# A graph layer's second sums: 31 of 49 blocks of counts as float32r in two 12-bit pieces, the rest as bf16 in three

## The chip, the cores and the metric
The kernel runs on one core of one Trainium2 chip. Its time is the device time of an execution in microseconds (us); lower is better. The engines are called as in the profile: PE (TensorE matmul) and PEld (its weight loads), DVE (VectorE), ACT (ScalarE), POOL (GpSimd) and SP (SyncE, which here only issues DMAs).

## The reference
Two graph layers on 6250 nodes of 128 features and 200,000 edges sorted by destination:

```python
h = relu(layernorm(x))
x = x + L0(h)      # mean aggregation, twice, then a layernorm
h = relu(layernorm(x))
x = x + L1(h)      # attention over the edges, with edge attributes
# inside L0, with agg(h) = segment_sum(h[src], dst) / max(count, 1)
h1 = relu(agg(h) @ W1l.T + h @ W1r.T + b1)
h2 = agg(h1) @ W2l.T + h1 @ W2r.T + b2
return layernorm(h2 + x) * gamma + beta
```

What matters here is the second aggregation, agg(h1) @ W2l.T. It is computed as agg(h1 @ W2l.T): a sum of 128 numbers over the edges of each node.

## The kernel before, in words
Nodes lie in 49 blocks of 128. The kernel has six stages, one after the other: front, count_sums, hidden, product_and_norm, attention, finish.

**Counts.** count_sums turns the edges into 62 slabs (NSL = N_BLK + NOV = 49 + 13; the 13 cover the edges that a block has beyond its share). A slab is a matrix of 49 blocks of 128 x 128 small integers, how often a source node of a block occurs among the edges of a destination; as bf16 it is 1568 KB. It is used for the first sums and stored in a_tab, a table in device memory.

**Second sums.** product_and_norm reads the slabs again and multiplies each block with that block's node sums. To keep float32 accuracy with bf16 matmuls, hidden splits each node's 128 values (po, in PSUM) into three bf16 pieces, SPL[:, h, 0..2], five DVE instructions for two blocks (finish, L1248 on). A slab is then 49 matmuls (L1666) with a block of counts as weights and the 3 x 128 columns of pieces moving, all adding into one PSUM bank of psR; DVE adds the three pieces up (rows, L1689), one reduction of 128 x 384 per slab.

The slabs live in two buffers A[0] and A[1]. SP loads a slab two ahead, in halves: blocks 0 to 24 (L1413) when PE has used these of the slab before last (s_hf), the rest (L1415) when PE is through with it (s_pr). In slabs 4 to 16 SP also stores a row block of r_tab (L1424) and waits until it has landed, before it goes on to the next slab.

Beside the 49 matmuls PE has small work at fixed places of a slab: at block 8 the transposes of edge terms (turn_edges, L1613), at 24 combine (slabs 1 to 13), at 30 the blocks of chunks (blocks_of_chunks, L1618 and L1619, which wait for GE of DVE's chunk_blocks) or the transposes of chunks (L1624), at 40 turn (L1595, waits for V) and weigh (L1603, waits for HT).

Destinations are normalized four blocks at a time. For the slab after such a quad (i == ends[q] + 1) DVE runs normed(q): it adds the overflow rows, means, statistics, then waits for ACT's square root, for ACT's U (norm, L1501), and for a second square root, before it reduces the slab. ACT then makes V (L1508). In the first 27 slabs, except these, DVE also computes an edge tile (edges, L1813 and L1816, four times each). POOL gathers the overflow rows and the chunks' rows, ACT also issues loads and stores of x.

Each engine runs its list strictly in the order written; semaphores order them against each other. attention gathers a row of x_tab for each edge on POOL (L1987), 15 chunks of 128 edges at a time.

Of the kernel before, what the change touches and what calls it, by code (L numbers as in the profile page):

```python
# [23 lines left out]
I16 = mybir.dt.int16  # L24
ACT = mybir.ActivationFunctionType
# [3 lines left out]
P = 128  # L29
# [5 lines left out]
QUAD = 4  # L35
# [39 lines left out]
UN_S, UNITS = 16, P // 16  # L75
NV = N_BLK * P
# [53 lines left out]
def build(nc, x, src, dst, edge_attr, W1l, W1r, b1, W2l, W2r, b2, gamma, beta,  # L130
          W, W_edge, att_src, att_dst, att_edge, bias, out):
    with ExitStack() as top:
# [20 lines left out]
        kinds[s_pq.num] = True  # L153

# [5 lines left out]
        ae_t = nc.dram_tensor("ae_t", [P, HEADS, NK], F32).ap()  # L160
        a_tab = nc.dram_tensor("a_tab", [NSL, P, N_BLK * P], BF16).ap()
# [12 lines left out]
        BLK = sb("BLK", [1, N_GRP + 2, 16], I16)  # L174
# [9 lines left out]
        ACC = sb("ACC", [P, NB, MW])  # L184
# [3 lines left out]
        W1T = sb("W1T", [P, 2, D_HID], F32, XS)  # L188
        W2T = sb("W2T", [P, 2, 2, D], F32, XS)
# [6 lines left out]
        identb = sb("identb", [P, P], BF16, XS)  # L196
        EKI = sb("EKI", [P, NPR + NOV], I32, XS)
        LEN = sb("LEN", [P, NPR + NOV], F32, XS)
        SECOND = sb("SECOND", [P, NPR], F32, XS)
        H = sb("H", [P, NB, XW], F32, XS)  # L200
        SPL = sb("SPL", [P, NB, 3, D], BF16, XS)
        lastp = sb("lastp", [P, 1], F32, XS)
        MB = sb("MB", [P, HEADS, D_EDGE], F32, XS)
        VAL = sb("VAL", [P, N_BLK, 4], F32, XS)
        OVI = sb("OVI", [P, N_BLK], I32, XS)
# [5 lines left out]
        flat_c = ACC[:].rearrange("p b f -> p (b f)")  # L211
# [21 lines left out]
        def front(at, block):  # L233
# [45 lines left out]
            zr = flat_c[:, NB * D:NB * D + 4 * P]  # L279
# [126 lines left out]
            def _(pool):  # L406
# [5 lines left out]
                pool.memset(zr, 0.0).then_inc(s_io, 1)  # L412
# [143 lines left out]
            def _(dve):  # L556
# [4 lines left out]
                dve.memset(BLK[:], 0)  # L561
# [171 lines left out]
        def count_sums(at, block):  # L733
# [246 lines left out]
            def _(dve):  # L980
# [39 lines left out]
                def rows(i):  # L1020
                    t = order[i]
                    if t < N_BLK:
                        to = ACC[:, t, 0:D]
# [17 lines left out]
                def behind(k):  # L1041
# [4 lines left out]
                    a = ACC[:, QUAD * k:high, 0:D]  # L1046
# [39 lines left out]
                dve.memset(ACC[:, N_BLK:, 0:D], 0.0)  # L1086
# [24 lines left out]
        stage(count_sums)  # L1111


        def hidden(at, block):
# [127 lines left out]
            def _(dve):  # L1242
                def mean(t, u):
                    dve.tensor_tensor(A2[:, u], ACC[:, bass.ds(t * PAIR, PAIR), 0:D],
                                      RCNT[:, bass.ds(t * PAIR, PAIR)][:, :, None].to_broadcast([P, PAIR, D]),
                                      ALU.mult).then_inc(s_a, 1)

                def finish(t, u):  # L1248
# [4 lines left out]
                    c.mark(dve.tensor_copy(SPL[:, pair, 0], o[:, :, 0]))  # L1253
# [4 lines left out]
                    dve.tensor_tensor(Y2[:, u], o[:, :, 0], SPL[:, pair, 0], ALU.subtract).then_inc(s_y, 1)  # L1258
                    dve.wait_ge(s_y, t + 3)
                    c.link(dve.tensor_copy(SPL[:, pair, 1], Y2[:, u]))  # L1260
                    c.mark(dve.tensor_tensor(SPL[:, pair, 2], Y2[:, u], SPL[:, pair, 1], ALU.subtract))
# [7 lines left out]
                def step(t, u):  # L1269
                    dve.wait_ge(s_t, t + 2)  # L1270
                    mean(t + 3, 1 - u)
                    finish(t, u)
                looped = (NP2 - 3) // HU * HU
                with dve.Fori(0, looped // HU) as i:
                    for u in range(HU):
                        step(HU * i + u, u % 2)
                for t in range(looped, NP2 - 3):
                    step(t, t % 2)
                for t in range(NP2 - 3, NP2):
                    finish(t, t % 2)  # L1280
# [5 lines left out]
        def product_and_norm(at, block):  # L1286
# [5 lines left out]
            s_hf = sem("q_hf", at)  # L1292
            s_gc = sem("g_c", at)
# [9 lines left out]
            s_pr = sem("q_pr", at)  # L1303
# [45 lines left out]
            rows3 = sb("rows3", [P, 2, 3, P], I32, at)  # L1349
            rowsf = sb("rowsf", [P, 3, P], F32, at)  # L1350
            dstf = sb("dstf", [P, P], F32, at)
            blk_row = sb("blk_row", [1, NK], I16, at)
# [6 lines left out]
            X = sb("X", [P, 3, QUAD, D], F32, at)  # L1359
# [39 lines left out]

            def width(q):  # L1400
# [6 lines left out]
            def _(sp):  # L1407
                for i, t in enumerate(order):
                    tile = a_tab[t].rearrange("p (h s) -> p h s", h=N_BLK)

                    if i >= 2:
                        sp.wait_ge(s_hf, i - 1)
                        sp.dma_start(A[i % 2][:, 0:HALF], tile[:, 0:HALF]).then_inc(s_ld[2 * (i % 2)], 16)  # L1413
                        sp.wait_ge(s_pr, i - 1)
                        sp.dma_start(A[i % 2][:, HALF:], tile[:, HALF:]).then_inc(s_ld[2 * (i % 2) + 1], 16)  # L1415
                    for n in range(KC):
                        if i == columns[n] + 6:
# [4 lines left out]
                    if 0 <= o < NOV:  # L1422
                        sp.wait_ge(s_rp, o + 1)
                        sp.dma_start(r_tab[o * P:(o + 1) * P], RP[:, o % 2]).then_inc(s_rt, 16)  # L1424
                        sp.wait_ge(s_rt, 16 * (o + 1))

# [1022 lines left out]
```

## Time and profile before

| | us |
|---|---|
| median of 3 runs | 4843.48 |
| lowest and highest | 4829.29, 4848.03 |
| span of the profiled execution, first to last instruction | 3640.9 |
| the second sums in it, first to last matmul (L1666) | 982.6 to 1539.8 |
| attention's gathers (L1987), from | 1557.05 |
| PE busy in the span | 3010.1 (83%) |
| DVE, POOL, ACT busy | 2616.2 (72%), 1928.6 (53%), 1004.4 (28%) |

The profiler gives the span from the first to the last instruction; it has no row for the rest of an execution's time. Matmuls are pipelined: the duration of one includes its way through the array, so their pace is read from the distance of their starts, or from a merged row as (duration - that of one) / (count - 1). Idle time ahead of an instruction stands in brackets with what ended it. The granted clock (PEclk) is 1.00 at 2.4 GHz and 0.50 at 1.2 GHz.

### The profile page before, as it was taken

To read this page: it belongs to the slowest core of one execution; us is meant where nothing else is said; L and a number is where in the kernel's file an instruction comes from. 1 tells how busy PE (TensorE), PEld (TensorE's weight loads), DVE (VectorE), ACT (ScalarE), POOL (GpSimd) and SP (SyncE) were. 2 spreads that over 40 slices of the span, in tenths; PEclk is the share of its full clock that TensorE was granted. 3 is DMA by queue.
4 is the path that set the end of the run, shared out by engine and by line. 5 is a ranking of instruction groups with operands and counts; after the bars stand their busy time and mean duration, and the time that the engine had idled before them with its cause. 6 is when DMAs were issued, how large, how long until landed. Compare 5 with 4: busy or idle time off the path is not lost. (4 is left out here: it accounts for less than half of the span.)

```text
span 3640.9 us, 66661 instructions
## 1 busy us (share of the span) xinstructions
PE 3010.1 (83%) x21816; PEld 2408.1 (66%) x21816; DVE 2616.2 (72%) x7465; ACT 1004.4 (28%) x2323; POOL 1928.6 (53%) x1970
## 2 busy tenths in 40 slices
PE   5799999999999999988777777777777777777774
PEld 5566666777765566567676666766666676666673
DVE  4789999996587644477676666676666676666677
ACT  4455555565300111122222212222222222211220
POOL 5430110162102233167777777777777777777773
PEclk9999999999999999967666666666666666666666
DMA  5233333474178788632222222222222222222225
GB/s 167 84 133 143 133 149 132 151 169 149 44 225 234 213 245 250 185 96 55 56 55 55 56 55 56 55 55 56 55 56 55 55 56 55 56 55 55 55 55 96
DMA packets 150358, 378.62 MB, mean 104 GB/s; under 512 B 38934, under 2 KB 87630, under 8 KB 141634
## 3 DMA queue, kind: packets, MB, share of 16 engines
q0 software_dynamic: 66640, 129.84, 17.8%
q1 hardware_dynamic: 41974, 217.22, 16.4%
q10 hardware_dynamic: 41372, 26.95, 2.5%
q8 instruction: 191, 3.13, 0.4%
q14 instruction: 181, 1.48, 0.1%
HBM read 255.77 MB, written 119.69 MB: 103 GB/s over the span
## 5 line engine op out<-in xcount | busy, mean ns | idle before, releaser
L1987 POOL DMA_INDIRECT G<-x_tab,idx x1611 | 1529.5, 949 | 501.4 <-issue 489.4
L2076 PE MATMUL pu<-MSG,OH 128*128 128x140 f32 x3282 | 626.6, 353 | 2.0 <-DVE ACC L2173 2.0
L2173 DVE TENSOR_TENSOR ACC<-pu,ACC 128x140 f32 x1641 | 485.2, 296 | 131.7 <-PE pu L2076 85.4
L931 PE MATMUL psR<-SPL,AE 128*128 128x384 bf16 x3038 | 569.5, 328 | 0.0
L2076 PEld LDWEIGHTS pu<-MSG,OH 128*128 128x128 f32 x3282 | 559.4, 246 | 5.5 <-DVE ACC L2173 2.0
L1666 PE MATMUL psR<-SPL,AE 128*128 128x384 bf16 x3038 | 511.9, 328 | 3.1 <-PEq L216 2.3
L2007 ACT COPY OHT<-pt 128x512 f32<-128x512 f32 (+1 forms) x432 | 236.9, 558 | 955.9 <-PE pt L2052 954.8
L898 ACT CAST AE<-psA 128x784 bf16<-128x784 f32 x496 | 397.6, 813 | 319.6 <-PE psA L921 318.2
L2065 PE MATMUL px<-ADG,OHT 128*128 128x4 f32 x3240 | 463.6, 270 | 0.0
L2065 PEld LDWEIGHTS px<-ADG,OHT 128*128 128x128 f32 x3240 | 435.6, 211 | 10.4
L1666 PEld LDWEIGHTS psR<-SPL,AE 128*128 128x128 bf16 x3038 | 297.7, 98 | 195.9 <-issue 7.4
L2098 PE MATMUL pc<-ident,L 128*60 128x128 f32 x108 | 42.2, 390 | 450.1 <-DVE L L2240 450.1
L1013 DVE TENSOR_TENSOR OHL<-iol,LH 128x1024 bf16<-128x1024 bf16 (+1 forms) x496 | 397.1, 801 | 22.6 <-PE psA L921 19.3
L931 PEld LDWEIGHTS psR<-SPL,AE 128*128 128x128 bf16 x3038 | 275.0, 98 | 146.2 <-issue 5.2
L2052 PE MATMUL pt<-ident,OH 128*128 128x128 f32 x1620 | 356.6, 381 | 11.0 <-ACT OHT L2007 9.2
L2098 PEld LDWEIGHTS pc<-ident,L 128*60 128x60 f32 x108 | 13.6, 126 | 482.9 <-issue 482.9
L2052 PEld LDWEIGHTS pt<-ident,OH 128*128 128x128 f32 x1620 | 284.1, 202 | 59.2 <-ACT OHT L2007 33.9
L921 PEld LDWEIGHTS psA<-OHH,OHL 128*128 128x128 bf16 x4800 | 234.5, 98 | 97.9 <-DVE OHH L1013 47.1
L921 PE MATMUL psA<-OHH,OHL 128*128 128x98 bf16 (+1 forms) x4800 | 262.4, 201 | 31.7 <-DVE OHH L1013 31.2
L1013 DVE TENSOR_TENSOR OHH<-iol,LH 128x784 bf16<-128x784 bf16 (+1 forms) x496 | 280.1, 565 | 0.0
L2233 DVE TENSOR_TENSOR L<-G,AE 128x60 f32<-128x60 f32 x108 | 27.8, 258 | 328.2 <-DMA G<-x_tab,idx 327.7
L853 POOL DMA_INDIRECT srows<-src_pad,EKI x38 | 51.1, 1344 | 397.9 <-DVE KB L996 343.7
(415 smaller groups left out, 3544.3 us busy)
## 6 DMA issues: line engine op xcount, KB each, us to landing
a_tab<-AE SPq DMA_DIRECT2D x62, 1568.0 KB
AE<-a_tab SPq DMA_DIRECT2D x60, 800.0 KB, 6.0
AE<-a_tab SPq DMA_DIRECT2D x60, 768.0 KB, 6.2
G<-x_tab,idx POOLq DMA_INDIRECT x1611
at_in<-in_edge_attr SPq DMA_DIRECT2D x26, 250.0 KB
room<-in_edge_attr ACTq DMA_DIRECT2D x24, 250.0 KB
ae_t<-room ACTq DMA_DIRECT2D x13, 256.0 KB, 5.4
AE<-ae_t SPq DMA_DIRECT2D x1, 3328.0 KB, 11.5
```

Source lines behind the costliest of these rows:

```text
L898: act.copy(A[i % 2][:, :, UN_S * u:UN_S * (u + 1)].rearrange("p h (k s) -> p k h s", k=2), psA[:, n % 2, :, 0:W8].rearrange("p k (s h) -> ...
L921: mm = pe.matmul(psA[:, n % 2, c * w // W8, to:to + w], OHL[:, n % 4, c], OHH[:, n % 4, c * step:c * step + w], start=True, stop=True)
L931: mm = pe.matmul(psR[:, i % 2, 0:3 * D], A[i % 2][:, h, :], SPL[:, h].rearrange("p s f -> p (s f)"), start=(h == 0), stop=(h == N_BLK - 1))
L1013: return dve.tensor_tensor(out.rearrange("p (s h t) -> p s h t", s=k, t=2), iol[:, 0:w].rearrange("p (h t) -> p h t", t=2)[:, None].to_bro ...
L1666: mm = pe.matmul(psR[:, i % 2, 0:3 * D], A[i % 2][:, h, :], SPL[:, h].rearrange("p s f -> p (s f)"), start=(h == 0), stop=(h == N_BLK - 1))
L1987: pool.indirect_dma_start(G[:, u % 4, j, :], None, x_tab, bass.IndirectOffsetOnAxis(ap=idx[:, u % 4, j:j + 1], axis=0)).then_inc(s_g[u % 4 ...
L2007: act.copy(OHT[:, 4 * n:4 * n + w, :].rearrange("p a b -> p (a b)"), pt[:, n % 2, 0:w * P]).then_inc(s_te, 1)
L2052: mm = pe.transpose(pt[:, n % 2, (j % 4) * P:(j % 4 + 1) * P], OH[:, u % 4, j, :], ident[:])
L2065: mm = pe.matmul(px_l[:, :, j], OHT[:, j, :], ADG[:, j, :], start=True, stop=True)
L2076: mm = pe.matmul(pu[:, k[0], k[1]:k[1] + MW], OH[:, u % 4, j, :], MSG[:, u % 2, j, :], start=True, stop=True)
L2098: pe.transpose(pl, L[:].rearrange("p h j -> p (h j)"), ident[:]).then_inc(s_lt, 1)
L2173: dve.tensor_tensor(a, pu[:, k[0], k[1]:k[1] + MW][:, None, :], a, ALU.add).then_inc(s_c, 1)
```

## The change
- hidden writes the pieces of the first 18 blocks as before (`three`, into SPB). For the other 31 it writes two pieces as float32r (`two`, into SPR): the value with its low 12 bits cleared, by shifts on the integer view, and the rest. Both have 12 bits of significand, so a product with a small integer is exact in either.
- product_and_norm: ACT casts the counts of blocks 18 to 48 from bf16 to float32r, in four groups a slab (7, 8, 8, 8 blocks), into one of three buffers AR. PE multiplies the blocks 0 to 17 as before (384 columns), the others from AR with 256 moving float32r columns; both add into psR. The order in a slab is six bf16 blocks, group 0, six, group 1, six, group 2, group 3, with the small work between them.
- The second half of a slab is now loaded when ACT has cast it; the first still waits for PE's s_hf, now behind block 17 and group 1.
- In the slab after a quad ACT puts the next slab's casts 0 and 1 between U and the second square root, and cast 2 between that and V.
- To make room, rows3 has one buffer, rowsf, X and zr lie elsewhere, ACC is split (SUMS before attention), and blk_row goes through a table blk_tab: 13 small stores on SP, one strided load and a memset on POOL at the start of attention. The four semaphores of attention's gathers are kept from the start of the kernel.

```diff
+N_BF = 18
+N_FR = N_BLK + N_BLK % 2 - N_BF
...
+                def two(t, u, r):
...
+                    o = po[:, u].rearrange("p (n l o) -> p n l o", n=PAIR, l=2)
+                    c = Chain(dve, own, t, 3)
+                    dve.wait_ge(s_o, t + 3)
+                    c.mark(dve.tensor_scalar(Y2[:, u].bitcast(I32), o[:, :, 0].bitcast(I32), 12, 12,
+                                             ALU.arith_shift_right, ALU.logical_shift_left))
+                    dve.wait_ge(s_b, t + 1)
+                    h = H[:, bass.ds(t * PAIR, PAIR), 0:D]
+                    c.link(dve.tensor_tensor(h, o[:, :, 1], h, ALU.add))
+                    pair = bass.ds(r * PAIR, PAIR)
+                    dve.tensor_tensor(SPR[:, pair, 1], o[:, :, 0], Y2[:, u], ALU.subtract).then_inc(s_y, 1)
+                    c.mark(dve.tensor_copy(SPR[:, pair, 0], Y2[:, u]))
...
+            groups = [range(N_BF, HALF)] + [range(h, h + 8) for h in range(HALF, N_BLK, 8)]
...
                         sp.wait_ge(s_hf, i - 1)
                         sp.dma_start(A[i % 2][:, 0:HALF], tile[:, 0:HALF]).then_inc(s_ld[2 * (i % 2)], 16)
-                        sp.wait_ge(s_pr, i - 1)
+                        sp.wait_ge(s_cs, 4 * (i - 1))
                         sp.dma_start(A[i % 2][:, HALF:], tile[:, HALF:]).then_inc(s_ld[2 * (i % 2) + 1], 16)
                     for n in range(KC):
+                        if i == columns[n] + 4:
+                            sp.wait_ge(s_bk, n + 1)
+                            sp.dma_start(blk_tab[:, n * P:(n + 1) * P], blk_row[:, n % 2]).then_inc(s_bs[n % 2], 16)
...
+                def cast(i, g):
+                    n = 4 * i + g
+                    if i >= 2 and g <= 1:
+                        act.wait_ge(s_ld[2 * (i % 2) + g], 16 * (i // 2))
+                    if n >= 3:
+                        act.wait_ge(s_cu, n - 2)
+                    rows_ = groups[g]
+                    act.copy(AR[:, n % 3, 0:len(rows_)], A[i % 2][:, rows_[0]:rows_[-1] + 1]).then_inc(s_cs, 1)
...
+                    normed = [q for q in range(NQ - 1) if i == ends[q] + 1]
+                    for q in normed:
+                        first_norm(q)
+                    if i + 1 < NSL:
+                        cast(i + 1, 0)
+                        cast(i + 1, 1)
+                    for q in normed:
+                        sqrt(2 * q + 1)
+                    if i + 1 < NSL:
+                        cast(i + 1, 2)
+                    for q in normed:
+                        second_norm(q)
...
+                def cast(i, g):
+                    n = 4 * i + g
+                    pe.wait_ge(s_cs, n + 1)
+                    for k, h in enumerate(groups[g]):
+                        mm = pe.matmul(psR[:, i % 2, 0:2 * D], AR[:, n % 3, k],
+                                       SPR[:, h - N_BF].rearrange("p s f -> p (s f)"), start=False,
+                                       stop=(h == N_BLK - 1))
+                    mm.then_inc(s_cu, 1)
...
+                    counted(i, range(0, 6))
+                    beside(i, 8)
+                    cast(i, 0)
+                    counted(i, range(6, 12))
+                    beside(i, 24)
+                    cast(i, 1)
+                    counted(i, range(12, N_BF)).then_inc(s_hf, 1)
+                    beside(i, 30)
+                    cast(i, 2)
+                    beside(i, 40)
+                    cast(i, 3)
...
-                    dve.wait_ge(s_pr, i + 1)
+                    dve.wait_ge(s_cu, 4 * (i + 1))
```

## Rows read from the trace of the kernel before

**Rows 1.** Stretches: busy us (instructions) per engine, PEclk, DMA share, GB/s
```profile
982.00:1121.00 139.00, 138.44 (x860) 85.87 (x861) 116.10 (x246) 0.00 (x0) 9.78 (x10) 0.99 0.70 228
1121.00:1234.00 113.00, 101.97 (x602) 62.12 (x600) 86.16 (x226) 11.66 (x30) 35.73 (x33) 0.95 0.79 216
1234.00:1541.00 307.00, 303.25 (x1913) 191.79 (x1911) 130.28 (x503) 39.84 (x98) 82.77 (x83) 1.00 0.80 231
1641.00:3550.00 1909.00, 1460.89 (x8993) 1317.26 (x8992) 1327.61 (x4391) 400.64 (x1334) 1445.11 (x1523) 0.68 0.25 55
```

**Rows 2.** Instructions of L1666: ns min/median/max, first and last start in us
```profile
L1666 PEld LDWEIGHTS psR<-SPL,AE x3038: 95/98/152, 982.5 to 1539.7; 128*128 128x128 bf16 x190
L1666 PE MATMUL psR<-SPL,AE x3038: 322/326/528, 982.6 to 1539.8; 128*128 128x384 bf16 x190
```

**Rows 3.** Waits, 982 to 1545: us in total, times, longest
```profile
DVE ACC L1689 <- PE psR L1666: 159.6, 32, 7.7
PE psg L1618 <- DVE GE L1774: 7.5, 10, 2.9
```

**Rows 4.** Timeline of PE, merged: start, us, operation, count, idle before
```profile
895.35 1.89 PE L1217 MATMUL po<-W2T,HID 128*128 128x256 f32 x8
897.07 0.27 PE L1199 MATMUL pt<-ident,A 128*128 128x128 f32 x1
897.18 0.27 PE L1200 MATMUL pt<-ident,H 128*128 128x128 f32 x1
...
1405.23 0.38 PE L1618 MATMUL psg<-dq,GE 49*128 49x2 f32 x2 [0.34 <-DVE GE L1774]
...
1417.31 10.89 PE L1666 MATMUL psR<-SPL,AE 128*128 128x384 bf16 x66
...
1584.57 3.41 PE L2065 MATMUL px<-ADG,OHT 128*128 128x4 f32 x30
```

**Rows 5.** Timeline of DVE, 1391 to 1427: reductions of four slabs
```profile
1391.29 0.56 DVE L1689 TENSOR_REDUCE ACC<-psR 128x128 f32<-128x384 f32 x1 [5.98 <-PE psR L1666]
...
1402.40 0.56 DVE L1689 TENSOR_REDUCE ACC<-psR 128x128 f32<-128x384 f32 x1
...
1418.97 0.56 DVE L1689 TENSOR_REDUCE ACC<-psR 128x128 f32<-128x384 f32 x1 [6.92 <-PE psR L1666]
...
1426.93 0.56 DVE L1689 TENSOR_REDUCE ACC<-psR 128x128 f32<-128x384 f32 x1 [5.97 <-PE psR L1666]
```

**Rows 6.** Instructions of L482 and of L1161, on ACT
```profile
L482 ACT CAST SPL<-H x7: 937/938/940, 59.4 to 102.4; 128x896 bf16<-128x896 f32 x7
L1161 ACT COPY H<-H x25: 400/402/405, 881.6 to 966.3; 128x256 f32 x20, 128x256 f32<-128x256 f32 x5
```

**Rows 7.** Timeline of ACT in the same period: the second square root
```profile
1401.47 0.30 ACT L1495 ACTIVATE sd<-nv,eps 128x4 f32<-128x4 f32 x1 [3.25 <-DVE nv L122]
```

**Rows 8.** DMA issues: count, KB each, median us from issue to landing
```profile
AE<-a_tab SPq DMA_DIRECT2D x60, 800.0 KB, 6.0
...
AE<-a_tab SPq DMA_DIRECT2D x2, 1568.0 KB, 8.1
```

**Rows 9.** Groups of DVE by line, 982 to 1121: busy us, mean ns
```profile
L1813 DVE TENSOR_TENSOR prod<-room,MB 125x512 f32<-125x512 f32 x64 | 44.1, 689 | 6.0 <-DMA room<-in_edge_attr 4.1 <-issue 0.3
```

**Rows 10.** Timeline of SP: issues of the r_tab store and of first halves
```profile
1053.07 0.78 SPq L1424 DMA_DIRECT2D r_tab<-RP  x1
1061.60 0.32 SPq L1413 DMA_DIRECT2D AE<-a_tab  x1
...
1069.61 0.32 SPq L1413 DMA_DIRECT2D AE<-a_tab  x1
```

**Rows 11.** Timeline of PE: weights that waited, and the matmuls behind them
```profile
1201.69 1.78 PE L1603 MATMUL pw<-WX,HT 128*128 128x136 f32 x8 [3.55 <-DVE HT L1729]
1203.27 15.60 PE L1666 MATMUL psR<-SPL,AE 128*128 128x384 bf16 x88
```

**Rows 12.** Costliest groups of the page: attention's gathers on POOL
```profile
L1987 POOL DMA_INDIRECT G<-x_tab,idx x1611 | 1529.5, 949 | 501.4 <-issue 489.4
```

More of the change, by code:

```diff
@@ L24 @@
 I16 = mybir.dt.int16
+F32R = mybir.dt.float32r
 ACT = mybir.ActivationFunctionType
@@ L153, in build @@
         kinds[s_pq.num] = True
+        s_src = [top.enter_context(nc.semaphore(f"row_g{u}")) for u in range(4)]
+        for h in s_src:
+            kinds[h.num] = True
         src_pad = nc.dram_tensor("src_pad", [E_PAD], I32).ap()
@@ L1111, in build @@
         stage(count_sums)
+        CS.close()
+        FS_ = ExitStack()
+        SPB = sb("SPB", [P, N_BF, 3, D], BF16, FS_)
+        SPR = sb("SPR", [P, N_FR, 2, D], F32R, FS_)
         def hidden(at, block):
@@ L1292, in product_and_norm @@
             s_hf = sem("q_hf", at)
+            s_cs = sem("q_cs", at)
+            s_cu = sem("q_cu", at)
+            s_bk = sem("q_bk", at)
+            s_bs = [sem(f"q_bs{k}", at) for k in range(2)]
             s_gc = sem("g_c", at)
@@ L1398, in product_and_norm @@
             LAST_I = NSL - 1
+            groups = [range(N_BF, HALF)] + [range(h, h + 8) for h in range(HALF, N_BLK, 8)]
+            assert len(groups) == 4 and groups[-1][-1] == N_BLK - 1
             def width(q):
@@ L1425, in _ @@
                         sp.wait_ge(s_rt, 16 * (o + 1))
+                for k in range(2):
+                    sp.wait_ge(s_bs[k], 16 * ((KC - k + 1) // 2))
             @block.gpsimd
@@ L1549, in _ @@
                 load(1)
+                for g in range(3):
+                    cast(0, g)
                 for i in range(NSL):
+                    cast(i, 3)
                     if i - 1 in at_tile:
@@ L1880, in attention @@
             assert N_GRP % UN == 0
-            s_g = [sem(f"a_g{u}", at, gathers=True) for u in range(4)]
+            s_g = s_src
             s_i = sem("a_i", at)
@@ L1978, in _ @@
                 sp.dma_start(AE[:], ae_t).then_inc(s_ael, 16)
+                sp.wait_ge(s_bz, 1)
+                with nc.allow_non_contiguous_dma(reason="groups of 15 numbers"):
+                    sp.dma_start(BLK[:, 2:N_GRP + 2, 0:J], blk_tab[:, 0:N_GRP * J].rearrange("o (g j) -> o g j", j=J)
+                                 ).then_inc(s_bl, 16)
             @block.gpsimd
@@ L1989, in step @@
                                 ap=idx[:, u % 4, j:j + 1], axis=0)).then_inc(s_g[u % 4], 16)
+                pool.memset(BLK[:], 0).then_inc(s_bz, 1)
                 steps(pool, step)
```

175 lines of the change are left out of this document (96 added, 79 removed).

## The prediction
> **What bounds the kernel now.** The change touches one stage in earnest, the second sums, so the profile is read there. First the stretches [rows 1]: the stage is cut where its load changes, and the reader should compare the engines within a row. From 982 to 1121 us (slabs 0 to 15) PE is busy throughout and DVE for 116 of 139. From 1121 to 1234 (slabs 16 to 26) PE has holes, DVE is at 76%. From 1234 to 1541 (slabs 27 to 61) PE is busy for 303 of 307, DVE for 42%. The DMA engines are busy 0.70 to 0.80 of it. Then the line view of the stage's matmuls [rows 2]: 3038, that is 49 for each of 62 slabs, starting at 982.6 and ending at 1539.8, 557 us. Last the waits [rows 3]: the reduction that closes a slab waits for PE 32 times, 160 us, while PE's longest item is 7.5 us. So PE bounds the stage, with DVE close behind while edge tiles last.
>
> **The price of a matmul.** The old form: 66 in 10.89 us, the last taking 0.33 to end, so (10.89-0.33)/65 = 0.1625 apart [rows 4]. A slab is 49 x 0.1625 = 7.96, also the step between two undisturbed reductions, 1418.97 to 1426.93 [rows 5]. The new form, float32r with 256 columns, is not in the trace. Nearest rows [rows 4]: float32 with 256 columns, issued as two matmuls each, (1.89-0.38)/7 = 0.216 apart, twice what 256 columns take at the pace of the 384; float32 transposes, 128 columns in one go, 0.11; float32 matmuls of only 4 columns, (3.41-0.27)/29 = 0.108. The last two, with 128 and 4 columns at the same step, show what a float32 weight load costs when nothing longer covers it. So one pass at a column a cycle gives 0.11 (columns 0.108, load 0.11, side by side); two cycles a column, as in each float32 pass, give 0.216; two such passes 0.432. I take 0.11, since cutting values to 12 bits only has a use if the form skips passes, and keep 0.216 as a rival; the gain cannot exceed that of 0.11.
> The Trainium skill (FP8 and Floating Point Precision, TensorE Precision Notes) has four passes for true float32 and a reduced-precision reading of it, cut to 22 bits; it does not name float32r nor its pace, and no row here shows it. If that reading is this form, a quarter of 2 x 0.216 is 0.108, the same sum.
> A new slab: 18 x 0.1625 + 31 x 0.11 = 2.93 + 3.41 = 6.34 us, 1.62 less. Times 62 that is 100 us, a ceiling. It is not reached, for a different reason in each stretch.
>
> **The casts.** ScalarE gets four per slab, of 896 and three times 1024 elements. Its nearest rows are a cast of 896, 0.938, and a copy of 256, 0.402 [rows 6]: 0.84 ns an element, 1.05 us for 1024, so 4.1 a slab, beside some 40 us of its own in the last 307 [rows 1]. Capacity is there. It runs in order, though, and has three buffers, so it is three groups ahead of PE at most, and around the normalization it is busy answering DVE. Bounds: nothing, or a cast behind V in each period, some 3 us.
>
> **Third stretch, a period of four slabs.** Now 1391.29 to 1426.93 = 35.65 us [rows 5]: 31.84 of counts, 3.8 of transposes, weights and small matmuls. Call the first reduction 0; PE then starts the slab of the normalization. New: that slab ends at 6.4. DVE's chain keeps its length: the second square root at 10.2 [rows 7], the next reduction at 11.1 [rows 5]. In the second slab PE comes to the blocks of chunks (L1618) at about 11.6, but GE is written after that reduction; today PE starts L1618 2.8 us after it and has waited 0.34 [rows 4, 5]. So it starts at 13.9, a stall of 2.3. The cast of group 2 (12.2), V (13.8) and the cast of group 3 (14.9) come under that cover. The slab ends at 16.9; the third, with weights and edge transposes, at 24.7; the fourth at 31.1. Period 31.4, gain 4.2.
> The same bytes move in less time: 0.80 of the stretch is busy DMA, so 0.85 or so of a full period, 30 us of 35.65; of 31.4 it would be 0.96. Half a tile lands 6.0 us after its issue, a whole one 8.1 [rows 8]; both halves are now asked for together at 72% of a slab, some 9 us ahead of need, enough while the queues are not full. Full gain is 4.2; queues held to 0.90 give a period of 33.8 and 1.9. I take 3.2, nearer the first because PE hardly waits for a tile now. Times 8.5 periods: 27 us.
>
> **First stretch.** Slabs take 8.5. DVE's 116.1/16 = 7.3 each is one floor, 5.5 of it the eight instructions of an edge tile [rows 1, 9]. SP's queue is the other. In slabs 4 to 16 SP asks for two halves, stores r_tab, and waits until that has landed behind their 1.6 MB: from the store at 1053.07 the next load is issued at 1061.60, and the next after that at 1069.61 [rows 10]. A turn of 8.0 to 8.9, whatever PE does. Those 13 slabs stay at 8.2, gain 0.3 each, 4; three before them gain 0.9; the first waits for its first cast. The blk_tab store adds an issue of 0.4 us on SP in some. In all 6 us.
> The Trainium skill (DMA: Bandwidth & Descriptors, Queues, rings and completion order) says that a semaphore increment lands only after every earlier write of that DMA engine. For this kernel r_tab would then wait for both halves in full; the 8.5 from 1053.07 to 1061.60 agrees, and a turn of 8.9 throughout would leave 2 of the 6.
>
> **Second stretch.** DVE sets its pace: three iterations in four hold an edge tile, the fourth the normalization (11.1 [rows 5]). Its slack is behind the weights, where PE stalls 3.55 for HT and then lost clock, 88 matmuls in 15.60 us instead of 14.6 [rows 11]. The group behind the weights becomes 0.88 from 1.47; PE's stall grows to 7 us and the clock is lost again. Gain 0.6 x 3, called 2.
>
> **Edits at little cost.** The hidden layer's DVE work shrinks (four instructions for five, 16 pairs), behind PE's matmuls of 0.216: nothing. BLK is loaded at the start of attention on SP, behind AE, while DVE clears its tiles; if that cover is gone DVE loses the lateness once. Its memset stands on POOL ahead of 1611 gathers, which at 949 ns and 0.30 of issue each make attention's length [rows 12]: +1 us (0 to 2). chunk_rows on POOL waits for rowsf of the chunk before, done two slabs before the wait in front of it: nothing. The load of X and the stores behind it on ScalarE's queue are issued up to two casts later, 2 us, with a period to spare.
>
> **The sum.** -27 -6 -2 +1 = -34 us, made on the profiled span, 3640.9 us. The median of the runs is 4843.5; the 1202.6 us between them lie around the span, no row shows them, and I hold them constant. 4843.5 - 34 = **4809.5**, 0.7% faster. A measurement of this kernel can tell about 0.5% (24 us) from no change.
>
> **Rivals.**
> 1. *The queues bind* (0.23). For it: 0.96 of the time in the sum above. Against it: PE hardly waits for tiles today. Third stretch 1.0 x 8.5, first 3, attention +1: 4833.
> 2. *Everything hides* (0.14). Queues give way, no stall but DVE's: third stretch 5.2 x 8.5 = 44, first 14, second 4, less 1: 4782.
> 3. *Two cycles a column* (0.10), on the slower side. A slab is 2.93 + 31 x 0.216 = 9.63, +1.67. Third stretch 34 x 1.67 = 57 and 5 of stalls; first, 16 x 1.7 = 27; second 10: +99, 4942. It decides from 0.163 per float32r matmul on. For it: each float32 pass of the trace. Against it: the use of the 12-bit cut.
> 4. *The clock* (0.06), also slower. In attention PE is busy for 1461 of 1909 us and has clock 0.68, in the third stretch 1.00 [rows 1]. Stalls in each period, and PE near 75% in the second stretch, could bring the lower level. A slab there costs up to twice 6.34, 4.7 more than now; the others gain 0.55, so it decides from 7 slabs of 62 on. With 20: 96 - 23 = +73, 4916.
> 5. *ScalarE is late* (0.05): 3 us more in each period: 4835.
>
> The forecast itself has 0.42, with 4795 to 4822 as its own range. The range for 8 in 10 reaches over rivals 2, 1 and 5: **4772 to 4856**. Faster by over 0.5%: 0.42 + 0.14 + the faster edge of rival 1 = 0.58; within 0.5%: 0.26; slower: rivals 3 and 4, 0.16.
>
> **What would show it.** Float32r matmuls 0.11 apart in PE's timeline (0.216: rival 3) and casts of 0.94 and 1.05 us. Reductions of the third stretch with a period near 32.4 and a stall at L1618's successor near 2.3; a period near 30 is rival 2, one of 34 with PE or ScalarE waiting for a_tab is rival 1. SP's turn in slabs 4 to 16 still 8 us or more. The second stretch as long as before. Attention the same within 2 us. It would be wrong most of all if the time around the span moved, or if the second sums lost their clock.

## The result and the profile after

| | us |
|---|---|
| before, median of 4 runs | 4836.39 (4829.00 to 4848.03) |
| after, median of 4 runs | 4800.85 (4794.29 to 4807.22) |
| ratio, with its 95% interval | 0.992 (0.990 to 0.994) |
| second sums after, first to last matmul | 1075.3 to 1603.3, 528.0 |
| second sums before [rows 2] | 557.3 |

The change is 0.8% faster, 35.5 us; 34 were forecast. The line view of the stage's matmuls, after (columns as in [rows 2]; L1742 are the bf16 blocks, L1750 the float32r ones), and below it ACT's casts:

```profile
L1750 PEld LDWEIGHTS psR<-SPR,AR x1922: 186/188/338, 1078.9 to 1603.2; 128*128 128x128 f32 x193
L1750 PE MATMUL psR<-SPR,AR x1922: 276/279/668, 1078.9 to 1603.3; 128*128 128x256 f32 x193
L1742 PE MATMUL psR<-SPB,AE x1116: 323/326/543, 1075.3 to 1601.4; 128*128 128x384 bf16 x186
...
L1561 ACT CAST AR<-AE x248: 920/1044/1054, 1078.0 to 1598.9; 128x896 fp32r<-128x896 bf16 x62, 128x1024 fp32r<-128x1024 bf16 x62
```

3038 matmuls as before, 31 of 49 in the new form. The three stretches of the stage after, in the form of [rows 1]:

```profile
1075.00:1221.00 146.00, 127.82 (x909) 102.33 (x909) 121.69 (x256) 66.46 (x68) 13.65 (x14) 0.98 0.67 226
1221.00:1326.00 105.00, 83.45 (x556) 66.99 (x557) 79.33 (x216) 53.81 (x74) 29.89 (x29) 0.93 0.83 224
1326.00:1603.00 277.00, 261.19 (x1905) 218.14 (x1904) 129.49 (x499) 172.05 (x233) 84.62 (x84) 0.98 0.84 255
```

PE, busy throughout the first stretch before, now has holes of 18 us in 146 there, though it has less to do: something else sets the pace. In the third it is still busy for 261 of 277. One period of the third stretch, the reductions in DVE's timeline (start, us; [rows 5] are their counterpart):

```profile
1402.92 0.56 DVE L1790 TENSOR_REDUCE SUMS<-psR 128x128 f32<-128x384 f32 x1 [4.73 <-PE psR L1750]
...
1414.04 0.56 DVE L1790 TENSOR_REDUCE SUMS<-psR 128x128 f32<-128x384 f32 x1
...
1421.38 0.56 DVE L1790 TENSOR_REDUCE SUMS<-psR 128x128 f32<-128x384 f32 x1 [4.55 <-PE psR L1750]
...
1429.77 0.56 DVE L1790 TENSOR_REDUCE SUMS<-psR 128x128 f32<-128x384 f32 x1 [5.97 <-PE psR L1750]
...
1436.32 0.56 DVE L1790 TENSOR_REDUCE SUMS<-psR 128x128 f32<-128x384 f32 x1 [4.49 <-PE psR L1750]
```

This period takes 33.4 us in place of 35.65; over seven periods the mean is 32.7. The 11.12 behind the first reduction is DVE's own chain, unchanged. PE's timeline in the slab behind it, merged as in [rows 4]:

```profile
1416.88 0.38 PE L1699 MATMUL psg<-dq,GE 49*128 49x2 f32 x2 [2.07 <-DVE GE L1875]
1417.12 0.47 PE L1700 MATMUL psg<-GE,ones 49*128 49x128 f32 x2
1417.52 1.26 PE L1750 MATMUL psR<-SPR,AR 128*128 128x256 f32 x8
1418.58 1.05 PE L1676 MATMUL pt<-ident,V 128*128 128x128 f32 x4
1419.28 2.06 PE L1750 MATMUL psR<-SPR,AR 128*128 128x256 f32 x8
```

Eight float32r matmuls take 1.26 us at the full clock; two microseconds behind the stall on GE they take 2.06, at the lower clock of 1.2 GHz. Last comes SP in the first stretch (issues of the two halves, L1462 and L1464, of blk_tab and of r_tab, L1476):

```profile
1142.19 0.32 SPq L1462 DMA_DIRECT2D AE<-a_tab  x1
1142.56 0.44 SPq L1464 DMA_DIRECT2D AE<-a_tab  x1
1143.04 0.43 SPq L1476 DMA_DIRECT2D r_tab<-RP  x1
1151.52 0.32 SPq L1462 DMA_DIRECT2D AE<-a_tab  x1
1151.88 0.43 SPq L1464 DMA_DIRECT2D AE<-a_tab  x1
1152.37 0.34 SPq L1468 DMA_DIRECT2D blk_tab<-blk_row  x1
1152.77 0.33 SPq L1476 DMA_DIRECT2D r_tab<-RP  x1
1160.83 0.32 SPq L1462 DMA_DIRECT2D AE<-a_tab  x1
```

A turn of SP, from one load of a first half to the next, is 9.3 us here; 8.5 of them lie between the r_tab store at 1143.04 and the next load at 1151.52. Over the 13 turns the mean is 8.9 us, in the change's second trace 8.6, and single turns take 6.6 to 10.3. The waits from 1105 to 1325 us name the victims (us in total, times, longest):

```profile
ACT AR L1561 <- DMA AE<-a_tab: 70.7, 29, 5.2
...
PE psR L1742 <- DMA AE<-a_tab: 10.0, 7, 3.0
```

**One table for all that follows**, in us, from each trace: the stage from first to last matmul, and the distance from the 4th reduction to the 17th, from the 17th to the 27th and from the 27th to the 61st. Slabs count from 0, so the first of these distances is the length of slabs 4 to 16, the ones with an r_tab store; in what follows the three columns are called the first, second and third stretch (they are nearly those of [rows 1], whose first also holds slabs 0 to 3). Where a kernel has more than one trace, all stand. The stage is the better measure of these edits: it is free of the other 4200 us.

| kernel | stage | 4 to 17 | 17 to 27 | 27 to 61 |
|---|---|---|---|---|
| before (three traces) | 557.3, 557.3, 563.1 | 110.8, 110.8, 110.8 | 105.0, 105.4, 110.6 | 298.1, 297.7, 298.2 |
| the change (two) | 528.0, 524.8 | 111.4, 107.9 | 105.0, 105.4 | 270.7, 270.8 |
| GE early | 512.5 | 105.7 | 106.9 | 259.1 |
| no landing wait | 516.4 | 99.7 | 101.8 | 274.1 |
| both (two) | 501.5, 504.5 | 102.2, 102.2 | 101.4, 104.6 | 257.3, 257.0 |
| no casts | 529.1 | 112.5 | 103.8 | 271.7 |
| three quarters of the bytes | 514.0 | 101.9 | 100.1 | 271.3 |
| one piece | 538.4 | 105.7 | 106.2 | 286.0 |
| both, 24 and 25 blocks | 506.2 | 101.2 | 103.6 | 260.0 |
| both edits on the kernel before | 555.8 | 110.8 | 108.2 | 293.4 |

In one and the same kernel the third stretch repeats within 0.5 us and the first within 3.5; the second moves by up to 5.6, so nothing is built on it. The kernels without casts, with three quarters of the bytes and with one piece leave out part of the sums; they are there for their traces, of which each has one.

### The profile page after: what moved, and what is told of

It reads as the page before. It is cut to its first block and busy times, and to the rows that moved or that the text cites. A ratio compares the mean times of both kernels' runs of the same rounds, so it can differ in the third digit from the quotient of the medians.

```text
span 4803.3 us, 67019 instructions
## 1 busy us (share of the span) xinstructions
PE 3358.5 (70%) x21816; PEld 2859.1 (60%) x21816; DVE 2595.9 (54%) x7447; ACT 1247.5 (26%) x2571; POOL 1920.3 (40%) x1971
## 5 line engine op out<-in xcount | busy, mean ns | idle before, releaser
L2175 PE MATMUL px<-ADG,OHT 128*128 128x4 f32 x3240 | 684.3, 324 | 422.3 <-issue 413.9
L2175 PEld LDWEIGHTS px<-ADG,OHT 128*128 128x128 f32 x3240 | 665.8, 296 | 410.0 <-issue 386.1
L2186 PEld LDWEIGHTS pu<-MSG,OH 128*128 128x128 f32 x3282 | 705.4, 303 | 7.4 <-DVE ACC L2283 2.3
L942 PE MATMUL psR<-SPL,AE 128*128 128x384 bf16 x3038 | 573.7, 330 | 0.0
L942 PEld LDWEIGHTS psR<-SPL,AE 128*128 128x128 bf16 x3038 | 276.1, 98 | 148.5 <-issue 8.8
L1750 PE MATMUL psR<-SPR,AR 128*128 128x256 f32 x1922 | 289.8, 296 | 11.6 <-ACT AR L1561 11.5
L1561 ACT CAST AR<-AE 128x896 fp32r<-128x896 bf16 x248 | 245.3, 1017 | 196.0 <-PE psR L1750 86.4
L1750 PEld LDWEIGHTS psR<-SPR,AR 128*128 128x128 f32 x1922 | 251.5, 193 | 27.5 <-ACT AR L1561 18.0
L2254 DVE TENSOR_TENSOR MSG<-G,pq 128x1920 f32<-128x1920 f32 (+1 forms) x109 | 231.7, 2126 | 16.8 <-issue 16.8
L2248 DVE TENSOR_TENSOR OH<-pq,REL 128x1920 f32<-128x1920 f32 x108 | 231.9, 2148 | 0.0
```

Of the source, the lines that this page charges most:

```text
L942: mm = pe.matmul(psR[:, i % 2, 0:3 * D], A[i % 2][:, h, :], SPL[:, h].rearrange("p s f -> p (s f)"), start=(h == 0), stop=(h == N_BLK - 1))
L1561: act.copy(AR[:, n % 3, 0:len(rows_)], A[i % 2][:, rows_[0]:rows_[-1] + 1]).then_inc(s_cs, 1)
L1750: mm = pe.matmul(psR[:, i % 2, 0:2 * D], AR[:, n % 3, k], SPR[:, h - N_BF].rearrange("p s f -> p (s f)"), start=False, stop=(h == N_BLK - 1))
L2175: mm = pe.matmul(px_l[:, :, j], OHT[:, j, :], ADG[:, j, :], start=True, stop=True)
L2186: mm = pe.matmul(pu[:, k[0], k[1]:k[1] + MW], OH[:, u % 4, j, :], MSG[:, u % 2, j, :], start=True, stop=True)
```

## The experiments

The theory: PE's shorter slabs brought out two waits that had cost the old kernel nothing, the one for GE behind DVE's chain in the third stretch, and SP's for the landing of r_tab in the first. The rivals are the DMA queues (bytes), ScalarE's casts, and the pace of the new form.

**The change again.**

> The changed kernel again, as it stands, to be compared with the three others of this call on the same chip. Expected 0.992 of the kernel before (35 us less), as in its first timing, with the second sums' third stretch at a period of 32.7 us and slabs 4 to 16 at 9.3 to 9.4 us for each turn of SP.

4803.68 us against 4837.71, ratio 0.993 (0.991 to 0.995). The third stretch repeats within 0.1 us, so differences of some us in it can be read. The first is 3.5 us shorter than in the first trace: SP's turn has a mean of 8.6 us, not the 9.3 to 9.4 expected.

**GE early.** DVE writes GE of the next chunk right after it has read this chunk's rows out of psg, ahead of the five instructions that make the keys and of that slab's other work.

```diff
-                    dve.tensor_tensor(LAST[:, k], dstf[:], psg[:, 3 * P:], ALU.not_equal)
+                    c.link(dve.tensor_tensor(LAST[:, k], dstf[:], psg[:, 3 * P:], ALU.not_equal))
+                    if n + 1 < KC:
+                        chunk_blocks(n + 1)
...
-                    for n in range(KC):
-                        if i == columns[n]:
-                            chunk_blocks(n)
+                    if i == columns[0]:
+                        chunk_blocks(0)
```

> GE is written as soon as DVE has read the transposed chunks out of PSUM, three instructions after the reduction instead of nine. Theory (DVE's late GE stalls PE in the second slab of a period): the stall of 2.1 us goes down to some 0.5, the lower clock behind it goes too, period 32.7 to about 30.7, so some 15 us less than the changed kernel. Rival (the DMA queues bind): period stays at 32.7. Rival (ScalarE is late): PE's stall moves to the cast of group 2 and at most 5 us are gained.

4784.07 us (4779.28 to 4788.42), 19.6 under the change; the stage is 12.3 to 15.5 us shorter (15 expected), the third stretch 11.7. PE's waits for GE in it, of the change and then of this kernel:

```profile
PE psg L1699 <- DVE GE L1875: 14.1, 7, 2.2
```

```profile
PE psg L1699 <- DVE GE L1875: 5.4, 7, 1.0
```

That is 8.7 us less. The change has three dips of the clock in that stretch, 3.4 us each at 1.2 GHz, which by an estimate at half the pace lose 1.7 us each; this kernel has none. 8.7 + 5.1 = 13.8, against 11.7 measured: a stall of 2 us costs itself and a dip now and then. The wait isn't gone, because GE still stands behind the reduction and three reads of psg; only the keys no longer come between.

**No landing wait.** Two semaphores for r_tab in place of one, so that SP need not wait for each store.

```diff
-            s_rt = sem("q_rt", at)
+            s_rt = [sem(f"q_rt{k}", at) for k in range(2)]
...
-                        sp.dma_start(r_tab[o * P:(o + 1) * P], RP[:, o % 2]).then_inc(s_rt, 16)
-                        sp.wait_ge(s_rt, 16 * (o + 1))
+                        sp.dma_start(r_tab[o * P:(o + 1) * P], RP[:, o % 2]).then_inc(s_rt[o % 2], 16)
...
```

> SP no longer waits for the landing of the r_tab store; two semaphores carry it to those who need it. Theory (SP's turn of 9.3 us bounds slabs 4 to 16): these slabs fall to DVE's floor of 7.1 to 7.6 us, about 22 us less than the changed kernel; the third stretch is unchanged. Rival (the queues' bytes bind there: 2.0 MB a slab): they stay above 8.8, at most 5 us less.

4785.62 us (4770.07 to 4796.37), 18 under the change. The first stretch takes 99.7, 8 to 12 less, or 7.7 a slab, where 7.1 to 7.6 and 22 us in all were expected. In these 99.7 us PE is busy for 96.6 and DVE for 93.4: both are near their limit, and PE's own work binds at least as much as DVE's. The third stretch, expected unchanged, is 3.4 us longer and has one dip of the clock more. ACT's and PE's waits for the table from 1105 to 1325 us:

```profile
ACT AR L1561 <- DMA AE<-a_tab: 35.8, 22, 2.6
...
PE psR L1742 <- DMA AE<-a_tab: 1.6, 1, 1.6
```

Half of ACT's wait for the table and nearly all of PE's is gone.

**Both.** The two edits together, and the same once more.

> Both edits of the two runs before together. If the two causes are separate the gains add: about 37 us less than the changed kernel, 0.984 to 0.985 of the kernel before. If the queues bind, less than the sum: 10 us or under.

> The version with both edits (GE early, no landing wait, 18 and 31 blocks) once more, in five rounds, since its timed gain over the change (26 us) was less than the 38 us that the two edits gave one by one, while its second sums had lost the whole 13 and 10 us. Theory: the stage holds 501 to 504 us and ends the last 34 slabs in 257, so the time is 56 us or more below the kernel before, a ratio of 0.988 where that takes 4806 to 4840 us and of 0.984 to 0.985 where it takes 3641. Rival: the two edits get in each other's way, then the gap to the kernel before stays under 50 us.

4777.47 us (4770.44 to 4783.65) against 4837.71, ratio 0.988 (0.986 to 0.990); the second time 4771.9 (4768.62 to 4780.85) against 4841.14, ratio 0.986 (0.983 to 0.989). The stage is at 501.5 and 504.5, 53 to 56 us under the kernel before, and in it the gains of the two edits simply add (12.3 to 15.5, and 8.4 to 11.6). Timed it is 60 and 69 us. This version beats both kernels. The expected 37 us under the change were too much: the stage gives 20 to 26, and 26 was measured. The 37 were the sum of the two timed gains, 19.6 and 18, and each of these is some us more than its stage shows; where the excess comes from is open.

**The kernel before, traced again.**

> The kernel before, profiled once more, since the first trace of it has a span of 3640.9 us and its timed runs are at 4836. If the profiled run was unlike the timed ones, the new span will be near 4830, with the difference in attention, whose groups took 18.7 us in the first trace and 28.9 in the changed kernel's. If the time lies around the span, the span stays at 3640. The second sums should take 557 us in either case.

The stage has 557.3 us a second time, to the tenth. Its span is 4764.2, so in length this execution is like the change's and not like the one that the prediction was made on. That is taken up below.

**No casts.** All casts but the first six are copies of one column; the counts of the float32r blocks are left out.

```diff
-                    act.copy(AR[:, n % 3, 0:len(rows_)], A[i % 2][:, rows_[0]:rows_[-1] + 1]).then_inc(s_cs, 1)
+                    if n < 6:
+                        act.copy(AR[:, n % 3, 0:len(rows_)], A[i % 2][:, rows_[0]:rows_[-1] + 1]).then_inc(s_cs, 1)
+                    else:
+                        act.copy(AR[:, n % 3, 0, 0:1], A[i % 2][:, rows_[0], 0:1]).then_inc(s_cs, 1)
```

> The casts are left out but for the first six; one column is copied in place of each, so the counts used for 31 blocks are wrong. Theory (casts are hidden under DVE's chain and GE's stall): third stretch 32.7 to 32 at most, first and second stretch unchanged. Rival (ScalarE late): period falls to 30 or less.

ACT's groups from 1070 to 1600 us: one cast now costs 0.19 us in place of 1.04, and the 242 short ones 42.9 us in all; the change's 248 casts take 247.0:

```profile
L1564 ACT CAST AR<-AE 128x1 fp32r<-128x1 bf16 x242 | 42.9, 189 | 356.7 <-PE psR L1753 180.4 <-DMA AE<-a_tab 153.2 <-issue 15.2
```

The stage stays: 529.1, the third stretch 271.7, and PE's waits for GE in it 13.6 us. 200 us of ScalarE's work are worth nothing in time. Rival 5 falls.

**Three quarters of the bytes.** The second half of a slab brings 12 of its 24 blocks; the others keep old counts.

```diff
-                        sp.dma_start(A[i % 2][:, HALF:], tile[:, HALF:]).then_inc(s_ld[2 * (i % 2) + 1], 16)
+                        sp.dma_start(A[i % 2][:, HALF:HALF + 12], tile[:, HALF:HALF + 12]).then_inc(s_ld[2 * (i % 2) + 1], 16)
```

> Each slab loads 37 of its 49 blocks; the other 12 keep what an earlier slab left, so sums are wrong. It takes a quarter of the bytes away. Theory: the third stretch keeps its period of 32.7 us within 0.7; SP's turn in slabs 4 to 16 falls from 9.3 to about 7.5, since the store lands behind fewer bytes. Rival (queues bind): the third stretch falls to 30 to 31.

The third stretch has 271.3, as with all bytes (270.7): rival 1 falls, the queues bind nothing there. The first stretch falls to 101.9, nearly as far as without the landing wait, which has all the bytes and takes 99.7. So the bytes cost time there only by way of SP's wait: what it waits for is the bytes ahead of r_tab's.

**One piece.** The float32r matmuls take 128 columns, the high piece alone; the low piece is left out of the sum.

```diff
-                        mm = pe.matmul(psR[:, i % 2, 0:2 * D], AR[:, n % 3, k],
-                                       SPR[:, h - N_BF].rearrange("p s f -> p (s f)"), start=False,
+                        mm = pe.matmul(psR[:, i % 2, 0:D], AR[:, n % 3, k],
+                                       SPR[:, h - N_BF, 0], start=False,
```

> The float32r matmuls take only the high piece, 128 columns instead of 256; the low piece is left out. It asks what sets their pace of 0.118 us. Weight load: still 0.11 to 0.118. Columns: 0.06. A form that is slow when short: 0.2 or more, and a slower stage.

PE's timeline of it: eight of the new form in 1.14 us, with their weights as in the change:

```profile
1396.47 1.14 PE L1750 MATMUL psR<-SPR,AR 128*128 128x128 f32 x8
...
1400.93 0.38 PE L1699 MATMUL psg<-dq,GE 49*128 49x2 f32 x2 [2.33 <-DVE GE L1875]
1401.17 0.47 PE L1700 MATMUL psg<-GE,ones 49*128 49x128 f32 x2
1401.57 1.39 PE L1750 MATMUL psR<-SPR,AR 128*128 128x128 f32 x8
1402.75 1.07 PE L1676 MATMUL pt<-ident,V 128*128 128x128 f32 x4
1403.48 1.95 PE L1750 MATMUL psR<-SPR,AR 128*128 128x128 f32 x8
```

The change takes 1.24 to 1.26 for eight. The median distance of starts is 0.113 us, for 0.118 with 256 columns: half the columns save 4%, so the second piece is all but free, and columns don't set the pace. Nor does each matmul have such a cost of its own: in the stage of the counts, with bf16 weights of the same 128 x 128, matmuls of 98 columns start 0.043 us apart in the median:

```profile
306.51 0.89 PE L921 MATMUL psA<-OHH,OHL 128*128 128x98 bf16 x16
```

Float32 with 4 and with 128 columns and float32r with 128 and with 256 all start 0.11 to 0.12 us apart ([rows 4] and here). That leaves the load of a float32 block of weights as what sets the pace.
And the kernel ends slower: the third stretch takes 286.0, 15 more than the change with twice the columns. The clock now falls behind each of the stretch's seven stalls on GE (the row at 1403.48), for 6.8 us each time, where the change has three falls of 3.4 us; in the whole stage it falls 17 times for 8 and 9 in the change. The stretch's granted clock is 0.90, the change's 0.98. The stalls on GE are nearly the same, 16.2 us in all for 14.1. Why the clock falls more often was not tried further.

**One size changed.** Both edits, with 24 and 25 blocks in place of 18 and 31 (`N_BF = 24`).

> The version with GE early and without the landing wait, but with 24 blocks in three bf16 pieces and 25 in two float32r pieces instead of 18 and 31. By the measured distances (0.1625 and 0.118 us) a slab costs 6 x 0.0445 = 0.27 us more. Theory: with both waits gone the stage follows PE's own work, so the last 34 slabs take 34 x 0.27 = 9 us more (257 to 266), the whole stage some 13 to 16 us more than 501.5 (about 516), the first stretch less than its full share, as DVE's edge tiles are near it. Rival: something else than PE's work sets the pace (queues, ScalarE's order): the stage stays within 3 us of 501.5. Another rival: a longer run of bf16 matmuls keeps the clock up better, then less than 9.

The stage takes 506.2, 2 to 5 more than the version with both edits, where 13 to 16 were expected; the third stretch 260.0, only 2.9 more, not 9. The reductions tell why. One period at 18 and 31 blocks, then at 24 and 25:

```profile
1384.39 0.56 DVE L1790 TENSOR_REDUCE SUMS<-psR 128x128 f32<-128x384 f32 x1 [4.63 <-PE psR L1750]
...
1395.52 0.56 DVE L1790 TENSOR_REDUCE SUMS<-psR 128x128 f32<-128x384 f32 x1
...
1400.50 0.56 DVE L1790 TENSOR_REDUCE SUMS<-psR 128x128 f32<-128x384 f32 x1 [2.21 <-PE psR L1750]
...
1408.45 0.56 DVE L1790 TENSOR_REDUCE SUMS<-psR 128x128 f32<-128x384 f32 x1 [5.53 <-PE psR L1750]
...
1415.00 0.56 DVE L1790 TENSOR_REDUCE SUMS<-psR 128x128 f32<-128x384 f32 x1 [4.56 <-PE psR L1750]
```

```profile
1296.76 0.56 DVE L1790 TENSOR_REDUCE SUMS<-psR 128x128 f32<-128x384 f32 x1 [4.90 <-PE psR L1750]
...
1307.88 0.56 DVE L1790 TENSOR_REDUCE SUMS<-psR 128x128 f32<-128x384 f32 x1
...
1312.87 0.56 DVE L1790 TENSOR_REDUCE SUMS<-psR 128x128 f32<-128x384 f32 x1 [2.21 <-PE psR L1750]
...
1321.09 0.56 DVE L1790 TENSOR_REDUCE SUMS<-psR 128x128 f32<-128x384 f32 x1 [4.14 <-PE psR L1750]
...
1327.97 0.56 DVE L1790 TENSOR_REDUCE SUMS<-psR 128x128 f32<-128x384 f32 x1 [4.90 <-PE psR L1750]
```

The third and fourth slab cost 0.27 and 0.33 more, the share that the pace gives. The first two take 11.1 + 5.0 in both: there DVE's chain and GE behind it hold PE, and the longer blocks fill what was a wait. In the third stretch PE's waits for GE fall from 5.3 to 0.6 us and those for casts from 1.7 to 0.3; of 34 x 0.27 = 9.2 us that leaves 3.1, beside 2.9 measured. With both edits in, half of the periods' slabs are DVE's, and a still cheaper matmul would win only in the other half.

**Both edits on the kernel before.** GE early as above; SP waits for the store of the slab before, not for its own, so that a store has a slab's time to land.

```diff
+                        if o:
+                            sp.wait_ge(s_rt, 16 * o)
                         sp.dma_start(r_tab[o * P:(o + 1) * P], RP[:, o % 2]).then_inc(s_rt, 16)
-                        sp.wait_ge(s_rt, 16 * (o + 1))
...
```

> The two edits on the kernel before: GE of a chunk written right behind the keys of the chunk before it, and SP waiting for the landing of the r_tab store of a slab earlier instead of its own. Theory: the change's shorter slabs made these two waits the bound, they cost the old kernel little. Then the third stretch gains the 0.34 us a period that PE waited for GE (3 us in all), slabs 4 to 16 at most 0.3 us each (4 us), the stage goes from 557 to 550 or more, and the timed gain is 3 to 8 us. Rival: the two waits bound the old kernel as much as the new: the stage falls by the 25 us that it fell in the new one, to about 532.

Ratio 0.9992 (0.998 to 1.000), 1.9 us, which is not clear of nothing; 3 to 8 were expected. The first stretch takes 110.8 with the landing wait and without it. The third gains 4.7 (3 expected). So the two waits were cheap there, and it is the change that made them dear: behind it the two edits are worth 20 to 26 us of the stage. And 110.8 in four traces of the old matmuls is PE's work. In the first trace of the kernel before PE has no idle time in slabs 4 to 16 (the first two numbers are the length of the window and PE's busy time):

```profile
1018.34:1129.19 110.85, 110.85 (x697) 69.34 (x696) 93.94 (x196) 0.00 (x0) 15.17 (x15) 1.00 0.73 238
```

**The kernel before, a third trace.**

> The kernel before once more, with its trace, to see which stretches of it change length from one execution to the next. The two traces of it so far agree on the second sums (557.3 us, first to last matmul) and differ outside: the stage of the counts 751 and 748 us, attention's groups of 15 chunks 18.7 and 28.9 us. The changed kernels' traces have all had 785 to 801 us in the stage of the counts. If that stage has two lengths by chance of the execution, this trace may show some 785 to 800 there. If the length belongs to the program, it is 748 to 751 a third time. Second sums 557 either way.

3643.36 us (3637.36 to 3645.78, 8 runs). The kernels timed beside it were of this short kind too: the one with both edits on the kernel before (3639.2), and the one with 24 and 25 blocks, which at 3595.0 is 46 us under the kernel before (3641.05). At all other times the kernel before took 4766 to 4856. The stage is 563.1 this time, not 557; all of the difference lies in the second stretch.
The question was whether the stage of the counts changes its length. From its first to its last matmul it has 729.7 us here, 729.7 and 727.5 in the two other traces of the kernel before, and 730.0 in the version with 24 and 25 blocks. In the nine traces of changed kernels of the long kind it has 761 to 778. Only one trace of the kernel before is of the long kind (the 727.5), so these traces can't tell whether the change lengthens that stage in this kind. Against it stands that the timed difference, 34 to 35.5 us, is no less than what the second sums alone give.

## Why the prediction was right, and where it was not

**The pace: right in kind, 7% off in size.** The matmuls start 0.118 us apart where 0.11 was taken; 31 x 0.008 = 0.25 us a slab. Rival 3 (0.216) is out. That the load of the weights sets the pace, with the columns hidden beside it, is what the one-piece kernel shows. The casts take 0.94 and 1.04 us, as predicted, and hide.
The passage of the Trainium skill on the reduced reading (FP8 and Floating Point Precision, TensorE Precision Notes) would have given an estimate of 0.108 for it, a quarter of what the four passes take in the trace, 2 x 0.216, if float32r is that reading, which it doesn't say. The measured 0.118 is near it, but that rule is not what sets it: at half the columns such passes would take 0.054, and the one-piece kernel has 0.113.

**Third stretch: right.** A gain of 27.4 (298.1 to 270.7), 27 predicted; a period of 32.7, 32.4 predicted; the stall on GE 2.07, 2.3 predicted. The dearer pace and the dips of the clock took about what had been set aside for the queues, so part of this is luck: by the chain alone, without the queues, 31.4 had been expected, and the queues did nothing (three quarters of the bytes change nothing).

**First stretch: the mechanism was right, a term was mis-sized.** SP's turn does bind behind the change, and slabs 4 to 16 gained nothing (they lost 0.6 us) or 2.9 in the two traces where 4 was predicted. The step that failed is "Those 13 slabs stay at 8.2": they took 8.6 and 8.3, and SP's turn had a mean of 8.9 and 8.6. The reading of [rows 10] was right as far as it went. The trace of the kernel before also has the landings: the store issued at 1053.07 landed at 1061.58, and the load followed at 1061.60; so it is in all 13 turns, with these times from issue to landing (least, median, most):

```profile
DMA to landing us min/median/max: 6.0/7.3/8.5
```

What the reading missed is that this wait did not set the length of the old slabs. PE did, with 8.52 a slab and no idle time, as the window above and the old kernel without the wait show; SP's turn, with a mean of 8.7 us, was about as long, and its loads ran two slabs ahead. [rows 1] already said it, with PE busy for 138.4 of 139 us. Behind the change PE's slabs are shorter; the first ones end 7.0 us apart, and once that lead is used up they follow SP.
The rule of the Trainium skill that a semaphore's increment lands behind the earlier writes of its DMA engine (DMA: Bandwidth & Descriptors, Queues, rings and completion order) agrees with these runs: in the kernel before, each of the 13 stores of r_tab landed 0.2 to 1.1 us after the second half issued ahead of it, never before it, and with fewer bytes in front the 13 slabs drop from 107.9 or more to 101.9. The turn of 8.9 throughout that was worked out by it, leaving 2 of 6 us, would have been the better sum.

**Second stretch: 2 predicted, none found**, within a scatter of 5. PE's stall on HT grew from 3.55 to 4.35 us (7 predicted) and PE lost the clock behind it, as was said:

```profile
1295.25 1.82 PE L1684 MATMUL pw<-WX,HT 128*128 128x136 f32 x8 [4.35 <-DVE HT L1830]
1296.71 2.07 PE L1750 MATMUL psR<-SPR,AR 128*128 128x256 f32 x8
```

**The clock (rival 4): in part.** The stage has 31 and 38 us at 1.2 GHz in the two traces of the change, 14 to 21 before. By an estimate at half the pace the 17 us more cost some 8, spread over single dips, most of 3.4 us. It stayed far from the 7 slabs from which it would have decided. (That rival's own sum has a slip: 20 slabs at 4.7 are 94, not 96.)

**The sum of the stage.** In the profiled execution -1.2 up to slab 3, +0.6, 0, -27.4 and -1.3 in the last slab make 29.3 us; in the second trace it is 32.5; 35 was forecast. The timed difference is 35.5 and 34, with an interval of some 29 to 49 us for the first. So that 34 and 35.5 are so close is partly luck: the stage gave 2 to 6 us less than its terms, and something outside it, or chance, gave them back.
What the change costs outside can be told from two traces of the short kind, the third of the kernel before and that of the version with both edits and 24 and 25 blocks, which contains the change. Between the last matmul of the counts and the first of the second sums it takes 103.7 us in place of 102.9, where nothing was predicted; from the last matmul of the second sums to the end 2103.3 in place of 2102.0 (2101.1 in the first trace), so attention is 1 to 2 us longer where +1 was predicted. Neither can have given the 2 to 6 us; where they come from is open.

**A step that was wrong, at no cost:** "the 1202.6 us between them lie around the span". Nothing lies around it: the profiled execution after has a span of 4803.3 and a time of 4805.1. The profiled execution before was of another kind than the runs it was set beside. The rows of POOL's gathers in 1700 to 3500 us, first of the kernel before in the trace of 3644 us, then in that of 4764 us, show where the time is:

```profile
L1987 POOL DMA_INDIRECT G<-x_tab,idx x1435 | 1363.6, 950 | 437.3 <-issue 437.3
```

```profile
L1987 POOL DMA_INDIRECT G<-x_tab,idx x938 | 889.8, 949 | 910.3 <-DVE MSG L2144 632.9 <-issue 277.4
```

One gather takes 0.95 us in both. In the first POOL waits for no other engine; in the second it waits 633 us for DVE, and gets through 938 in place of 1435. The second sums have the same length in the first two traces, one of either kind (557.3 and 557.3), so the sum over their rows held, and only the words about the rest were false. A table that shows a span 1200 us short of the time should have been read as two kinds of execution, and attention's terms as unknown for the timed one.

## What to carry to other kernels

Before an engine's work is made cheaper, list the waits that end just before it is ready, and price them at the new length: here two of them, all but free before, took 20 to 26 of the some 55 us that the new matmuls had to give, and a few moved lines gave them back. Where one queue carries large loads and a small store whose landing is waited for, that wait lasts as long as the loads do. And ask of every wait in the old kernel whether it set the time: the wait for the landing was there in all 13 turns and cost nothing, since PE never stood idle. The busy time of the bounding engine in that stretch tells it, and so does the wait's removal on the old kernel.

## What the runs showed of the hardware

- float32r with 256 moving columns starts every 0.118 us at the full clock and every 0.213 at 1.2 GHz, with 128 columns every 0.113 and 0.213. The load of its weights sets it (188 ns by the row, for bf16 98), not the columns: bf16 with 98 columns starts every 0.043 us.
- Fewer columns can be slower: at 128 in place of 256 the stage lost 10 to 14 us. PE spent 109 us of it at 1.2 GHz, against 31 to 38 in the change.
- A store of r_tab issued behind the two halves of a slab on the same queue landed 6.0 to 8.5 us after its issue, and 0.2 to 1.1 us after the second half.
- The same program takes 3637 to 3648 us or 4766 to 4856. All timed runs on one chip were of the short kind, all on three others of the long kind; whether the chip is the reason is not shown. In the longer kind PE, DVE and ACT stand still for stretches, of which at least the first part lies under POOL's indirect DMAs: from 1737.9 to 1748.3 us of the 4764 us trace they are busy for 1.1, 1.7 and 1.6 of 10.4 us. Single matmuls start 1 to 3 us apart while POOL issues a group of gathers (its last one at 1742.79), and merged ones follow behind it:

```profile
1740.83 0.17 PE L2065 MATMUL px<-ADG,OHT 128*128 128x4 f32 x1 [1.97 <-issue]
1743.61 0.17 PE L2065 MATMUL px<-ADG,OHT 128*128 128x4 f32 x1 [2.62 <-issue]
1745.01 0.37 PE L2065 MATMUL px<-ADG,OHT 128*128 128x4 f32 x1 [1.24 <-issue]
...
1748.59 4.43 PE L2065 MATMUL px<-ADG,OHT 128*128 128x4 f32 x20
```

  A group of 15 gathers takes 1800 x 15/938 = 28.8 us so, 1800 x 15/1435 = 18.8 otherwise. What holds them was not tried and stays open. It is by far the largest thing in this kernel's time, 1100 us or more, and outside the change.
